# Windowed attention on one core: exponentials of the moved block ahead of PSUM copies, the other block first in the value product, and x loaded in two halves

## What is computed

```python
qkv = (x @ Wqkv + bqkv).reshape(B, S, 3, H, Dh)
kwin = jnp.concatenate([kp[:, :, :-2], kp[:, :, 1:-1], kp[:, :, 2:]], axis=3)
vwin = jnp.concatenate([vp[:, :, :-2], vp[:, :, 1:-1], vp[:, :, 2:]], axis=3)
scores = jnp.einsum('bhnqd,bhnkd->bhnqk', qb, kwin) * scale
scores = jnp.where(mask[None, None], scores, jnp.float32(-1e+30))
attn = jax.nn.softmax(scores, axis=-1)
out = jnp.einsum('bhnqk,bhnkd->bhnqd', attn, vwin)
return out @ Wout + bout
```

## Time and profile before

| | |
|---|---|
| median of 3 runs | 2595.36 us |
| profiled execution | 2599.21 us, of which the span from first to last instruction is 2597.4 us |
| PE busy | 2464.5 us, 95% |
| PE weight loads busy | 2034.7 us, 78% |
| DVE busy | 1589.0 us, 61% |
| ACT busy | 1493.8 us, 58% |
| DMA, 1120 to 2540 us | 71% of the 16 engines' time, 185 GB/s |

### The profile page before, as it was taken

The page is one execution under the profiler, slowest core; times in us unless marked ns, Lnnn a source line. Parts: engine busy times, 40 slices in busy tenths (PEclk is TensorE's granted clock), DMA queues, the critical chain, the costliest instruction groups (busy, mean ns, idle before and its releaser), DMA issues.

```text
span 2597.4 us, 57215 instructions
## 1 busy us (share of the span) xinstructions
PE 2464.5 (95%) x20512; PEld 2034.7 (78%) x20512; DVE 1589.0 (61%) x4395; ACT 1493.8 (58%) x3748; POOL 339.0 (13%) x595
## 2 busy tenths in 40 slices
PE   6999999999999999989999999999999999999997
PEld 4788888888888888867777777777778778778885
DVE  5444444444444444347777777777777777777774
ACT  6333333333333333337777777777777777777774
POOL 0011111111111111021111111111111111111111
PEclk7999999999999999999999999999999999999998
DMA  4422222222222222125777776777777777777765
GB/s 177 154 82 82 81 81 81 81 81 81 81 77 74 74 76 77 41 82 147 192 196 188 189 191 175 204 181 182 191 195 195 191 189 180 198 181 204 185 189 144
DMA packets 587918, 366.78 MB, mean 141 GB/s; under 512 B 21760, under 2 KB 542976, under 8 KB 587184
## 3 DMA queue, kind: packets, MB, share of 16 engines
q1 hardware_dynamic: 587552, 363.68, 51.1%
q0 software_dynamic: 144, 0.17, 0.0%
HBM read 197.04 MB, written 166.72 MB: 140 GB/s over the span
## 4 chain that ended last, share of the span: by engine, by line
PE 43%; DMA 6%; issue 4%; ACT 2%; SPq 1%; DVE 1%; POOLq 0%; POOL 0%
PE job_ps L1158 11%; PE job_ps L1176 7%; PE job_ps L1270 6%; PE pT_ps L1243 6%; PE job_ps L1167 6%; PE score_ps L1229 5%; DMA turned_blocks<-wqkv_raw 3%; DMA wqkv_raw<-turned_blocks 3%; ACT wqkv_raw L967 1%; SPq L880 1%; PE pT_ps L1248 1%; DVE wqkv_raw L1062 0%; PE job_ps L1290 0%; PE score_ps L1280 0%; DVE k_lo L1087 0%
## 5 line engine op out<-in xcount | busy, mean ns | idle before, releaser
L967 ACT ACTIVATE wqkv_raw<-wqkv_raw,neg_max 128x384 f32<-128x384 f32 (+1 forms) x1024 | 622.4, 609 | 183.9 <-DVE neg_max L1045 181.8
L494 ACT ACTIVATE relu<-up_ps,fc_scale 128x512 f32<-128x512 f32 x256 | 176.2, 688 | 658.1 <-PE up_ps L625 658.1
L1045 DVE CUSTOM_DVE_ANT_0 wqkv_raw<-score_ps,mask 128x384 f32<-128x384 f32 (+1 forms) x1024 | 503.5, 547 | 46.3 <-PE score_ps L1229 44.6
L568 DVE SCALAR_TENSOR_TENSOR sq<-up_ps,relu 128x512 f32<-128x512 f32 x256 | 177.0, 691 | 533.5 <-ACT relu L494 532.1
L635 PE MATMUL down_ps<-proj_T,sq_hi 128*128 128x512 f32 x1024 | 409.4, 400 | 0.9 <-DVE sq_lo L551 0.9
L637 PE MATMUL down_ps<-proj_T,sq_lo 128*128 128x512 f32 x1024 | 403.7, 394 | 0.0
L621 PE MATMUL up_ps<-f_xT_hi,fc_T 128*128 128x512 f32 x1024 | 400.2, 391 | 1.4 <-DVE low L539 1.4
L623 PE MATMUL up_ps<-f_xT_lo,fc_T 128*128 128x512 f32 x1024 | 400.1, 391 | 0.0
L1062 DVE STREAM_TRANSPOSE wqkv_raw<-wqkv_raw 128x384 f32<-128x384 f32 (+1 forms) x512 | 289.4, 570 | 170.4 <-ACT wqkv_raw L967 158.1
L977 ACT COPY pT<-pT_ps 128x384 f32<-128x384 f32 (+2 forms) x512 | 271.5, 530 | 146.9 <-PE pT_ps L1243 137.3
L1158 PE MATMUL job_ps<-xT_hi,wqkv_hi 128*128 128x256 f32 x1024 | 330.9, 323 | 0.1
(11 more groups left out here) (131 smaller groups left out, 4202.0 us busy)
## 6 DMA issues: line engine op xcount, KB each, us to landing
turned_blocks<-wqkv_raw SPq DMA_DIRECT2D x124, 768.0 KB, 4.7
wqkv_raw<-turned_blocks SPq DMA_DIRECT2D x496, 192.0 KB, 3.6
xT_hi<-xT SPq DMA_DIRECT2D x65, 256.0 KB, 4.8
xT_lo<-xT SPq DMA_DIRECT2D x65, 256.0 KB, 5.2
f_x_in<-in_L_attn_x SPq DMA_DIRECT2D x64, 256.0 KB, 3.2
xT<-f_xT_hi SPq DMA_DIRECT2D x64, 256.0 KB, 2.6
xT<-f_xT_lo SPq DMA_DIRECT2D x64, 256.0 KB, 2.8
part_in<-in_L_attn_x SPq DMA_DIRECT2D x64, 256.0 KB, 3.5
```

The lines of the kernel that those rows point to most:

```text
L568: nc.vector.scalar_tensor_tensor(sq[:, s % 2, :], up_ps[:, s % 2, :], 0.0, relu[:, s % 2, :], ALU.max, ALU.mult).then_inc(sq_done, 1)
L967: nc.scalar.activation(probs[:, u, cols], probs[:, u, cols], ACT.Exp, bias=neg_max[:, u:u + 1], scale=-1.0, accum_out=prob_sum[:, u:u + 1] ...
L1045: nc.vector.tensor_tensor_reduce(out=probs[:, u, cols], in0=score_ps[:, h, cols], in1=mask[:, cols], scale=-SCORE_SCALE, scalar=3e38, op0= ...
```

## The change

It has three parts. On ScalarE the order "copy 0, exp 0, copy 1, exp 1, copy 2, exp 2, copy 3, exp 3" becomes "exp 0, copy 0, exp 1, copy 1, exp 2, exp 3, copy 2, copy 3". On TensorE the value product does block 1 first (it reads `pT`, the PSUM copies), and waits for the moved block (`blocks_moved`) only ahead of block 0's 24 matmuls. On SyncE the four DMAs of `load_x` are split: the two of the high part stay in iteration c = 1, the two of the low part go to iteration c = 0 of the next tile.

```diff
-            def load_x(j):
+            def load_x(j, low):
...
-                if c == 1 and i + XR - 1 < NT:
-                    load_x(i + XR - 1)
+                if c == 0 and 1 <= i < NT - XR + 2:
+                    load_x(i + XR - 2, 1)
+                if c == 1 and i + XR - 1 < NT:
+                    load_x(i + XR - 1, 0)
...
-                for h in range(HC):
+                for h in range(HC // 2):
+                    if t < STEPS:
+                        exp(t, 0, h)
                     if 1 <= t <= STEPS:
                         copy_pT(t - 1, h)
+                for h in range(HC // 2, HC):
                     if t < STEPS:
                         exp(t, 0, h)
+                for h in range(HC // 2, HC):
+                    if 1 <= t <= STEPS:
+                        copy_pT(t - 1, h)
...
-                pe.wait_ge(blocks_moved, 16 * STRIPS * (t + 1))
                 pe.wait_ge(pT_done, HC * (t + 1))
-                for b in range(2):
+                for b in (1, 0):
+                    if b == 0:
+                        pe.wait_ge(blocks_moved, 16 * STRIPS * (t + 1))
```

More of the change, by code:

```diff
@@ L843, in _ @@
         def _(sp):
-            def load_x(j):
+            def load_x(j, low):
                 if j >= XR - 1:
                     sp.wait_ge(job_filled, A_NUMBER[4 * (j - XR) + 5])
[L848 to L852, removed]
+                xT = xT_lo if low else xT_hi
+                for r in range(1 if j < 0 else 0, 2):
+                    blk = (2 * j + 1 + r) % NBLK
+                    sp.dma_start(xT[:, :, x_slot(j) + r, :].bitcast(F32), xT_rows(xT_dram, blk, low)).then_inc(
+                        x_here[j % XR], 16)
             def load_part(i, b):
@@ L887, in _ @@
             for j in range(-1, XR - 1):
-                load_x(j)
+                for low in range(2):
+                    load_x(j, low)
             sp.wait_ge(wout_lo_done, 1)
```

## The result

The changed kernel takes 2529.84 us (median of 4 runs, 2526.69 to 2532.66) against 2594.24 us before: ratio 0.9751, 95% interval 0.9734 to 0.9768. That is 64.4 us less, where 38 was forecast; 2529.84 lies 0.2 us under the range. The profiled execution took 2528.54 us, with a span of 2526.7.

A forecast was written before the change was run, and what follows sets the result against it. PE was taken to wait for the moved block's DMA chain. A tile of 2 x 11.02 + 2 x 10.53 = 43.10 us, 10.78 an iteration against 11.09, saves 39 us, 38 after adjustments: 2557 us median, range 2530 to 2588.

The forecast's parts named there:

- What bounds the kernel now: PE needs about 10.54 us an iteration and waits for the moved block's DMA chain; 0.55 of 11.09 us is pause.
- Part 1, the chain: With exponentials first on ScalarE, the moved block goes out 1.04 us earlier, S + 5.4 after first scores (S) instead of S + 6.5.
- Part 1, the loop of ACT and DVE: From one first maximum (m) to the next: q's high part at m + 4.90, loop 10.42 us, or 11.02 with `add_out`.
- The allowance for late blocks: 0.02 us an iteration for tiles worse than the noisy one, 2 or 3 us in all; bounds none and 0.1.
- the 1 us allowed for it: The first tile has no `add_out`, so its iterations last at most 10.53: 4 x 0.25 = 1 us more gained.
- The sign given for being wrong: If iterations c = 1 and 2 of a tile last 10.5 us, the loop of ACT and DVE does not bind.
- The tie of PE to m: Through k's low part at m + 6.69 and 2.99 us to the next scores: next m at least m + 10.53.
- PE's own work is the bound: Rival: all pauses go, 10.54 us an iteration, 70 us less, 2525; 12 in 100.
- The wake-up after copy 3: PE's delay from copy 3 to the value product: 0.05 us taken; 0.25 would add 0.12 to two iterations of four.
- Part 2: Value product with block 1 first: the moved block may land 0.78 us later without a pause; nothing is added.
- Part 3: Loads of x in halves: each delays the next block 0.83 us, where four together cost 1.66; bounds 0 and 1.66 each.
- The clock: Rival: clock falls from 2.4 to 1.2 GHz for one projection 40 times, costing 120 us against 38 gained, 2677; 2 in 100.

The follow-up runs named there:

- e6_mix: The changed kernel with ScalarE's copies 0 and 1 ahead of exp 0 and exp 1 again (exp 2, exp 3 still ahead of copies 2, 3): 2509.62 us.
- e7: The changed kernel with VectorE's `add_out` behind the four maxima of block 0 instead of ahead of them: 2511.55 us.

## Why the prediction was wrong

**What bounds the kernel now: right.** PE waited for the chain of the moved block, and with the chain hidden the time fell by 64 us. The idle row fell from 81.7 to 5.2, "some 10" was said. (Not all of the 0.55 us over a quiet iteration was pause: see the clock below.)

**Part 1, the chain: right.** The block goes out at S + 5.33 and S + 5.72 in iterations 61 and 62 (1803.20 and 1814.03 less the first scores), S + 5.4 and S + 5.9 were said.

**Part 1, the loop of ACT and DVE: right mechanism, and the step that failed is its size.** The prediction put q's high part at "m + 4.90 (the sum above)" and with it the loop at 10.42 and 11.02 us. The timeline of ACT in iteration 42, one with `add_out`, whose first maximum starts at 1597.89 (m):

```profile
1598.47 0.62 ACT L970 ACTIVATE wqkv_raw<-wqkv_raw,neg_max 128x384 f32<-128x384 f32 x1 [1.65 <-DVE neg_max L1054]
...
1599.08 0.46 ACT L980 COPY pT<-pT_ps 128x384 f32<-128x384 f32 x1
1599.44 0.62 ACT L970 ACTIVATE wqkv_raw<-wqkv_raw,neg_max 128x384 f32<-128x384 f32 x1
...
1600.05 0.46 ACT L980 COPY pT<-pT_ps 128x384 f32<-128x384 f32 x1
1600.41 0.62 ACT L970 ACTIVATE wqkv_raw<-wqkv_raw,neg_max 128x384 f32<-128x384 f32 x1
...
1601.02 0.61 ACT L970 ACTIVATE wqkv_raw<-wqkv_raw,neg_max 128x384 f32<-128x384 f32 x1
...
1601.63 1.05 ACT L980 COPY pT<-pT_ps 128x512 f32<-128x512 f32 x2
1602.57 0.48 ACT L996 ACTIVATE q_hi<-job_ps,qk_bias 128x256 fp32r<-128x256 f32 x1
```

An exponential is followed by a copy after 0.61 us and not 0.66, a narrow copy by an exponential after 0.36 and not 0.38, a wide one by the next after 0.47 and not 0.49. Three times 0.05 and the rest make m + 4.68: 0.22 us less, once in each loop. The other terms of the loop came out as said, in the timeline of DVE in the same iteration:

```profile
1603.45 0.48 DVE L1092 SCALAR_TENSOR_TENSOR q_lo<-job_ps,qk_bias,q_hi 128x256 fp32r<-128x256 f32 x1 [1.06 <-ACT k_hi L999]
...
1604.25 0.55 DVE L1054 CUSTOM_DVE_ANT_0 wqkv_raw<-score_ps,mask 128x384 f32<-128x384 f32 x1
...
1607.67 0.51 DVE L1085 TENSOR_TENSOR oT_lo<-oT,oT_hi 128x256 fp32r<-128x256 f32 x1
...
1608.71 0.54 DVE L1054 CUSTOM_DVE_ANT_0 wqkv_raw<-score_ps,mask 128x384 f32<-128x384 f32 x1
```

That is 0.88, 0.80, 3.42 and, with `add_out`, 1.04 us; from first maximum to first maximum the loop takes 10.82 us where 11.02 was said. The 0.66 was read in the earlier trace rows where the copy waited for PE's transposes: they end at 1614.00 (1613.51 and 0.49), the copy starts at 1614.03. One iteration on, where ACT is late, the kernel before itself has 0.61 (1624.13 to 1624.74). e6_mix shows the same within one kernel. Timeline of ACT, iteration 41 (first maximum at its usual place) and iteration 42 (late):

```profile
1582.79 0.62 ACT L970 ACTIVATE wqkv_raw<-wqkv_raw,neg_max 128x384 f32<-128x384 f32 x1
...
1583.46 0.48 ACT L980 COPY pT<-pT_ps 128x384 f32<-128x384 f32 x1
...
1593.31 0.62 ACT L970 ACTIVATE wqkv_raw<-wqkv_raw,neg_max 128x384 f32<-128x384 f32 x1
...
1593.93 0.46 ACT L980 COPY pT<-pT_ps 128x384 f32<-128x384 f32 x1
```

In the first the second head's transposes end at 1583.42 (the row of PE is 1582.93 with 0.49), the copy follows 0.04 later, and the distance is 0.67; in the second ACT itself is late, the transposes are done, and it is 0.62. A spacing of 0.66 with no idle time noted beside it was a wait of some 0.05 us. In the kernel before the narrow copies had 132 us of idle before them, put down to PE, so the order that I took the spacings from was paced by PE.

What this one term does, counted from first scores to first scores: the iterations with `add_out` came out at 10.75 and 10.78 where 11.02 was said, the others at 10.37 and 10.44 where 10.53 was said. A tile is 42.34 us and not 43.10; 0.19 us an iteration, 24 us in all. (In c = 0 and 1 PE's own work takes over as the limit before the whole 0.22 is gained.) The allowance for late blocks (2 to 3 us) wasn't needed either. 38 + 24 + 3 = 65 of the 69 us by which the stage of the profiled execution shrank. The other 4 lie at the stage's ends: the first tile took 39.75 us, where 42.34 less the 1 us allowed for it would be 41.34, and the last three iterations 29.64 (2465.03 to 2494.67), where the middle's 10.37, 10.44 and 10.75 make 31.56. The sign given for being wrong, "iterations c = 1 and 2 last 10.5", came half true, 10.44 and 10.75: counted from first scores, the late first maximum lengthens the iteration that it stands in, c = 2 and 3.

**The tie of PE to m: right, and its floor was wrong.** "PE alone needs about 10.54 us" came from iteration 41, in which no pause is noted. The projection there starts 7.55 us after the scores; in the changed kernel's iteration 41, where k's low part is done 0.2 us sooner, it starts after 7.44 (1593.64 less 1586.20), and e6_mix has iterations of 10.36 to 10.44. The tenth was a wait as well: in the kernel before k's low part ended at 1619.16, 0.06 us ahead of the projection at 1619.22. The rival "PE's own work is the bound" gave 2525, close to what was measured, and it did not happen: the changed kernel was bound by the loop in two of four iterations, and e6 and e7 took the last 20 us out to reach the bound by PE, at 2510.

**The wake-up after copy 3: dearer than taken, but it never decided anything.** In the changed kernel's c = 2 and 3 the product starts 0.14 us after copy 3 ends (median), where 0.05 was taken; the wait for k's low part, behind it, ends later all the same. In iteration 42 the product starts 0.77 us after the scores of block 1, in iteration 41 0.73 (timeline of PE, first scores of iteration 41 at 1586.20 and of 42 at 1596.64):

```profile
1591.46 0.45 PE L1238 MATMUL score_ps<-k_hi,q_hi 32*128 32x384 f32 x4
...
1592.19 0.86 PE L1280 MATMUL job_ps<-pT,values 128*32 128x128 f32 x24
...
1593.64 0.50 PE L1185 MATMUL job_ps<-wout_hi,oT_hi 128*128 128x512 f32 x1
...
1599.60 0.55 PE L1252 MATMUL pT_ps<-ident,wqkv_raw 128*128 128x128 f32 x3
...
1602.05 0.45 PE L1238 MATMUL score_ps<-k_hi,q_hi 32*128 32x384 f32 x4
...
1602.82 0.86 PE L1280 MATMUL job_ps<-pT,values 128*32 128x128 f32 x24
```

PE meets the late copies already at the third head's transposes, 2.96 us after the first scores (1599.60), right when copy 0 ends (1599.08 and 0.46); S + 2.9 was the estimate for a quiet iteration. The scores of block 1 are late by that, and the product with them.

**Part 2: right.** Alone it takes off 35 of the 81.7 us idle before the moved block.

**Part 3: right in sign, the price too high.** 0.83 us was taken for each half. The block behind the high half lands in 4.64 us and the one before it, behind the low half, in 4.61, where 5.45 was the time with no load ahead in the earlier trace rows. That 5.45 was a slow one: the mean at that place in the kernel before is 4.67, so the four loads cost 1.36 us on the mean (6.03 less 4.67) and a half some 0.2. What the working left out is the read-back beside the low half, 0.46 us longer.

**The clock.** The changed kernel has no iteration at the low level between its first tile and its last; the rival did not occur. But the kernel before was not at full clock throughout, as the prediction read it: a slice of the page, 65 us long, is too coarse to tell. Iterations 22, 39, 55 and 91 of the kernel before, each as one stretch (us, then busy times, then the granted clock, share and rate of DMA):

```profile
1395.75:1409.70 13.95, 12.07 (x124) 9.99 (x124) 8.90 (x29) 8.19 (x24) 2.95 (x6) 0.88 0.74 191
1587.30:1601.19 13.89, 12.04 (x126) 10.10 (x125) 8.90 (x28) 8.19 (x24) 2.93 (x6) 0.88 0.72 189
1766.82:1781.12 14.30, 12.01 (x125) 9.85 (x124) 8.88 (x28) 8.11 (x23) 2.62 (x5) 0.88 0.70 192
2169.40:2182.15 12.75, 10.46 (x123) 8.79 (x122) 9.24 (x29) 8.20 (x24) 2.18 (x4) 1.00 0.65 172
```

In the first three the clock fell from 2.4 to 1.2 GHz for a part of the iteration, right after PE had paused 1.88, 1.85 and 2.29 us before the value product. The fourth had the same pause of 2.29 us and kept the full clock, and so did three more with pauses of 2.07 to 2.13; what decides is open. The third and fourth differ by 1.55 us, so the three falls cost an estimated 4.7 us, which went with the pauses and which the prediction counted as pause. The rule of the Trainium skill ("TensorE: Matmul & The Clock Gate", section A second HAM failure mode: psum-queue depth-cycling), that frequent micro-pauses make the clock oscillate, is not what is seen here: the kernel before paused in most iterations and its clock fell in three, each time after a long pause.

**Occupancy.** The Trainium skill ("Perfetto Trace Analysis", section Identifying the Most-Contended Engine) has the engine with the highest occupancy optimized first, for TensorE with the share of its weight loads as the measure. That was PE before and after, with 78 and 80% by weight loads and 95 and 98% by matmuls, and PE did end as the limit. But the share did not show where the last 20 us were: they came from moving two copies ahead of two exponentials on an engine that was 58% busy, and it was the sum of the starts around the loop that showed this.

## What to carry to other kernels

When several engines run hand-written orders, add up each closed loop of starts (here from a first maximum to the next) beside each engine's work, since hiding one wait makes the next longest loop the limit; an instruction that can run early belongs in front of one that will wait. Take the spacings for such a sum from a place where the engine runs behind its suppliers: a start that falls within some 0.05 us of its supplier's end may be a wait, even if no idle time is noted. And once a wait is hidden, go back over what was done to hide it: here half of the new order on ScalarE was enough for the chain, and the other half cost 20 us.

## What was not expected of the hardware

The same copy of 128x384 out of PSUM is recorded with 0.48 us where it had just waited and with 0.46 where ACT was running behind (mean 477 ns over the kernel before, 460 over the changed one). The out-transfer behind two loads of x took hardly longer than one without (means 4.85 and 4.65 us in the changed kernel), while behind four it took 6.03 on the mean of the kernel before: the cost of a burst ahead of a transfer was not in proportion to its bytes. That the two shorter bursts had time to drain before the block was issued fits (the issues stand 4.33 us apart, 1809.70 to 1814.03, against 2.40 from the last pair of four to the block in the earlier trace rows), but no run measures it by itself.
